# One program for the folded attention and the preparation of the quantised layers, with two loops in another order

## The reference, cut to what matters

```python
def _L1_xattn_ref(x, context, w_qkv, w_proj, b_proj):      # 16 heads of 8 channels; 257 context keys + 32 own
    q, k, v = split(x @ w_qkv.T)
    extra_k, extra_v = split(context)
    k = concatenate([extra_k, k]); v = concatenate([extra_v, v])
    attn = softmax((q * scale) @ k.T)
    return (attn @ v) @ w_proj.T + b_proj

def _L2_attn_ref(x, Wq, bq, Wk, bk, Wv, bv, temperature):
    q = (x @ Wq + bq).reshape(b, h, dh, t)                  # a reshape without a transpose: the "folded" layout
    k = (x @ Wk + bk).reshape(b, h, dh, t)
    v = (x @ Wv + bv).reshape(b, h, dh, t)
    attn = softmax(einsum('bhdt,bhds->bhts', k, v) * temperature)
    return einsum('bhdt,bhts->bhds', q, attn).reshape(b, t, d)

def _L2_ffn_ref(x, w1, b1, w2, b2):
    def _quant_per_tensor(x):
        scale = max(max(abs(x)), 1e-6) / 127                # one scale for the whole tensor
        return round(x / scale), scale
    def _qlinear(x2d, w, b):
        xq, sx = _quant_per_tensor(x2d); wq, sw = _quant_per_tensor(w)
        return (xq @ wq.T + b) * (sw * sx)
    return _qlinear(gelu(_qlinear(x, w1, b1)), w2, b2)
```

## Time and profile before

| | |
|---|---|
| three runs, us | 3599.93, 3603.46, 3603.1; median 3603.1 |
| the profiled execution's own time, us | 3595.71 |
| its span, first to last instruction, us | 3593.9 |
| busy, share of the span | PE 90%, DVE 70%, ACT 51%, POOL 35% |
| granted TensorE clock, mean | 0.933 |

### The profile page before, as it was taken

How to read it: one execution, slowest core, us unless ns; L and a number is a source line. 1 busy time by engine, 2 the same in 40 slices (tenths; PEclk the granted TensorE clock), 3 DMA queues, 4 the chain that set the end, 5 groups by cost and what they waited for, 6 DMA issues and landing times. The chain is left out here.

```text
span 3593.9 us, 110060 instructions
## 1 busy us (share of the span) xinstructions
PE 3239.3 (90%) x41584; PEld 2701.9 (75%) x41584; DVE 2516.7 (70%) x7222; ACT 1816.6 (51%) x4562; POOL 1252.0 (35%) x1855
## 2 busy tenths in 40 slices
PE   6887999999899999888899999999999999774866
PEld 4666999999867777546789899988998899543345
DVE  6785999999868888567455555555555555477765
ACT  4332777787677777574433333333333333224463
POOL 4774888888733333204200000000000000155042
PEclk8996999999999999998799999999999999877677
DMA  4001000000022222100465555555555555264000
GB/s 120 8 2 39 1 0 0 0 0 0 4 80 77 79 77 79 44 1 7 99 148 126 130 134 128 132 130 133 126 129 137 126 133 130 67 107 71 0 3 27
DMA packets 375654, 254.59 MB, mean 71 GB/s; under 512 B 118724, under 2 KB 371608, under 8 KB 374680
## 3 DMA queue, kind: packets, MB, share of 16 engines
q1 hardware_dynamic: 370968, 245.64, 28.1%
q10 hardware_dynamic: 4352, 4.20, 0.5%
HBM read 233.73 MB, written 15.75 MB: 69 GB/s over the span
## 5 line engine op out<-in xcount | busy, mean ns | idle before, releaser
L2477 PE MATMUL psum<-L_xattn_ctxT,L_xattn_q_ctx 128*128 128x257 f32 x2048 | 508.6, 388 | 2.5 <-issue 2.0
L1076 PE MATMUL psum<-L_ffn_share,L_ffn_prob 128*128 128x128 f32 x4096 | 488.1, 278 | 22.9 <-DVE L_ffn_prob L1009 15.4
L893 POOL TENSOR_TENSOR L_ffn_sums<-L_ffn_sims 128x1024 f32<-128x1024 f32 x256 | 485.4, 1913 | 61.2 <-DVE L_ffn_prob L1009 61.2
L2508 PEld LDWEIGHTS psum<-L_xattn_probT,L_xattn_ctx 32*128 32x128 f32 x16384 | 469.1, 187 | 44.5 <-issue 42.0
L1076 PEld LDWEIGHTS psum<-L_ffn_share,L_ffn_prob 128*128 128x128 f32 x4096 | 471.4, 193 | 35.7 <-DVE L_ffn_prob L1009 25.5
L2508 PE MATMUL psum<-L_xattn_probT,L_xattn_ctx 32*128 32x128 f32 x16384 | 493.5, 273 | 2.1 <-DVE L_xattn_probT L2391 2.1
L2329 ACT ACTIVATE L_xattn_prob<-psum,L_xattn_nmax 128x258 f32<-128x258 f32 x512 | 239.1, 472 | 478.1 <-DVE L_xattn_nmax L2377 461.1
L2300 POOL TENSOR_TENSOR L_xattn_z_var<-L_xattn_z_mv,L_xattn_z_eps 128x1 f32<-128x1 f32 x32 | 6.1, 192 | 1244.7 <-DVE L_xattn_z_mv L2403 1215.4
L2477 PEld LDWEIGHTS psum<-L_xattn_ctxT,L_xattn_q_ctx 128*128 128x128 f32 x2048 | 367.2, 190 | 64.4 <-issue 7.9
L935 ACT ACTIVATE psum<-L_ffn_sums,L_ffn_bias 128x512 f32<-128x512 f32 x512 | 339.1, 686 | 64.8 <-DVE L_ffn_prob L1009 60.3
L1009 DVE SCALAR_TENSOR_TENSOR L_ffn_prob<-L_ffn_sums,L_ffn_best,psum 128x512 f32<-128x512 f32 x512 | 358.1, 741 | 7.0 <-ACT psum L935 3.4
(11 more groups left out here) (461 smaller groups left out, 6521.8 us busy)
## 6 DMA issues: line engine op xcount, KB each, us to landing
L_xattn_ctx<-ctx_dram SPq DMA_DIRECT2D x512, 256.0 KB, 3.7
L_xattn_ctxT<-ctx_T_dram SPq DMA_DIRECT2D x128, 257.0 KB, 3.3
L_xattn_k_all<-ctx_T_dram SPq DMA_DIRECT2D x128, 128.5 KB, 2.1
L_xattn_v_all<-ctx_dram SPq DMA_DIRECT2D x128, 128.0 KB, 2.2
L_attn_qkv_scratch<-L_attn_qkv SPq DMA_DIRECT2D x24, 256.0 KB, 2.9
L_attn_rows<-L_attn_qkv_scratch SPq DMA_DIRECT2D x24, 256.0 KB, 5.3
start_raw<-ctx_dram ACTq DMA_DIRECT2D x16, 256.0 KB, 12.0
L_xattn_v_rows<-L_xattn_v SPq DMA_DIRECT2D x8, 256.0 KB, 2.3
```

What stands on the lines that cost most here:

```text
L893: nc.gpsimd.tensor_tensor(sums[:, h % RING, :, :], sx, sy, ALU.add).then_inc(summed, 1)
L1076: last = nc.tensor.matmul(pair(2 * s)[:, c * P:(c + 1) * P], prob[:, h % RING, c * P:(c + 1) * P], share[:, h % RING, :], start=(h == 0 an ...
L2477: last = nc.tensor.matmul(scores(s)[:, g, 0:CTX], q_ctx[:, p, c, b, h:h + 4, :].rearrange("p h n -> p (h n)"), ctxT[:, b, c, :], start=(c ...
L2508: last = nc.tensor.matmul(mix_bank(r)[:, c * P:(c + 1) * P], ctx[rows, b, k, c * P:(c + 1) * P], probT[rows, b % 2, k, :, :].rearrange("p ...
```

## The change

Four things are edited.

1. In `context_attention` TensorE's `turn` is split in `turn_upper` and `turn_lower`, and `mix_values` of the sequence before stands between them.
2. In `folded_attention`'s projection TensorE issues the transpose of a tile ahead of the matmul of the tile before it. The normalisation moves from VectorE to ScalarE, and GpSimd makes one more operand for it (mean times inverse deviation, negated).
3. What `quantised_ffn` did ahead of its first layer moves into `folded_attention`'s program, in a class `QuantisedFront`. The weights are loaded at its start; peaks and bias parts are made in the projection's last step, the rounding of the weights between the two loops; the six small transfers stand in SyncE's queue between `store_res(1, 1)` and `load_back(0, 0)`, their load after the loop over pairs.
4. At the end VectorE adds the results in five groups (8, 8, 8, 4, 4 tiles), each followed by its moments; GpSimd, ScalarE and the peaks follow by the same groups. The tile `back` is now a part of `qkv`.

```diff
@@ context_attention, TensorE @@
-                    turn(t, b)
+                    turn_upper(t, b)
                     if b:
                         mix_values(t, b - 1, before)
                     elif before:
                         mix_values(t - 1, BT - 1, before)
+                    turn_lower(t, b)
...
+class QuantisedFront:
+    PARTS = (range(0, 8), range(8, 16), range(16, 24), range(24, 28), range(28, 32))
...
+    def sp_send_parts(self, sp):
+        H, C = self.H, self.C
+        sp.wait_ge(self.parts_done, 3)
+        for i in range(3):
+            sp.dma_start(self.bias_dram[i:i + 1, 0:H].rearrange("a (p j) -> (a p) j", j=C), self.b_part[:, i, 0:C]).then_inc(
+                self.parts_out, 16)
+            sp.dma_start(self.bias_dram[i:i + 1, H:H + D].rearrange("a (p j) -> (a p) j", j=1),
+                         self.b_part[:, i, C:self.N_BIAS]).then_inc(self.parts_out, 16)
...
+    def sp_load_parts(self, sp):
+        sp.wait_ge(self.parts_out, 96)
+        sp.dma_start(self.bq[:, :], self.bias_dram).then_inc(self.bq_in, 16)
+
+    def pool_factors(self, pool):
+        for part in self.PARTS:
+            self.front.pool_rstd(pool, 0, only=part)
+            self.front.pool_shift(pool, self.shifted, part).then_inc(self.centred, 1)
...
@@ folded_attention @@
-        back = sb("back", [P, TILES, D])
+        back = qkv[:, :, 0, :]
...
             store_res(1, 1)
+            quant.sp_send_parts(sp)
             load_back(0, 0, back_in)
...
+            quant.sp_load_parts(sp)
             for n in (STEPS - 2, STEPS - 1):
                 store_res(n, n % 2)
-                load_back(n - 1, 1 - n % 2, back_in)
+                load_back(n - 1, 1 - n % 2, mid_in if n == STEPS - 1 else back_in)
             load_back(STEPS - 1, 1, last_in)
...
-            def rstd(t, j, live):
+            def normal_factors(t, j, live):
                 if live(-1):
-                    front.pool_rstd(pool, t + 1 - (j + 1) % W, only=(j + 1) % W)
+                    s = (j + 1) % W
+                    front.pool_rstd(pool, t + 1 - s, only=s)
+                    pool.drain()
+                    nc.gpsimd.tensor_scalar(shifted_mean[:, s:s + 1], front.mv[:, s, 0:1], front.rstd[:, s, :], -1.0, ALU.mult,
+                                            ALU.mult).then_inc(centred, 1)
...
@@ folded_attention, ScalarE @@
             def turn_copy(t, j, live):
-                front.act_copy(act, t - j, only=j)
+                if live(0):
+                    front.act_copy(act, t - j, only=j)
+                if live(-1):
+                    s = (j + 1) % W
+                    act.wait_ge(centred, t + 2)
+                    nc.scalar.activation(front.xn[:, s, :], core.x[:, ds(t + 1, 1), :].rearrange("p a d -> p (a d)"),
+                                         ACT.Identity, bias=shifted_mean[:, s:s + 1],
+                                         scale=front.rstd[:, s, :]).then_inc(front.normed, 1)
...
@@ folded_attention, VectorE @@
-                if live(-1):
-                    front.dve_normalise(dve, t + 1 - (j + 1) % W, only=(j + 1) % W)
...
+                if not live(-2) and live(-1):
+                    quant.dve_weight_peaks(dve)
+                    quant.dve_split_bias(dve)
...
             pipelined(dve, W, -1, 1, project)
+            quant.dve_greatest(dve, 1, 3, 1)
+            quant.dve_steps(dve, 1, 3, 1)
+            quant.dve_round_weights(dve)
             pipelined(dve, W, 0, 2, step)
-            dve.wait_ge(back_in, 16 * (STEPS - 1))
-            most = slice(0, TILES - S)
-            nc.vector.tensor_tensor(core.x[:, most, :], core.x[:, most, :], back[:, most, :], ALU.add)
+            dve.wait_ge(back_in, 16 * (STEPS - 2))
+            for part in quant.PARTS[0:3]:
+                add_back(part[0], part[-1] + 1)
+                quant.dve_moments(dve, part)
+            dve.wait_ge(mid_in, 16)
+            add_back(TILES - 2 * S, TILES - S)
+            quant.dve_moments(dve, quant.PARTS[3])
+            quant.dve_peak(dve, 0)
             dve.wait_ge(last_in, 16)
-            rest = slice(TILES - S, TILES)
-            nc.vector.tensor_tensor(core.x[:, rest, :], core.x[:, rest, :], back[:, rest, :], ALU.add)
+            add_back(TILES - S, TILES)
+            quant.dve_moments(dve, quant.PARTS[4])
+            for k in range(1, len(quant.PARTS)):
+                quant.dve_peak(dve, k)
+            quant.dve_step_x(dve)
...
@@ folded_attention, TensorE @@
+                if live(0):
+                    front.pe_transpose(pe, t - j, only=j)
                 if live(1):
...
-                if live(0):
-                    front.pe_transpose(pe, t - j, only=j)
...
             pe.wait_ge(qkv_done, TILES)
+            quant.pe_greatest(pe, 1, 3, quant.peaks_w, 1)
+            pe.wait_ge(quant.steps_read, 1)
             pipelined(pe, W, 0, 3, step)
-
-
+            pe.wait_ge(res_done, TILES)
+            quant.pe_greatest(pe, 0, 1, quant.peaks_x, 2)
```

More of the change, by code:

```diff
@@ L2900, in turn_copy @@
                 nc.scalar.copy(qT[:, j, :, :], bank_a(j).rearrange("p (c w) -> p c w", c=C)).then_inc(hT_done, 1)
-            for k, c in enumerate(chunks):
-                act.wait_ge(centred, k + 1)
-                for t in c:
-                    front.act_normalise(act, shifted, t)
             pipelined(act, W, 0, 0, gelu)
```

274 lines of the change are left out of this document (136 added, 138 removed).

## The result

| | before | after |
| --- | --- | --- |
| median of the runs, us | 3601.5 (3594.4 to 3603.5, 4 runs) | 3560.5 (3558.7 to 3565.2, 4 runs) |
| the profiled execution's own time, us | 3595.71 | 3560.66 |
| its span, us | 3593.9 | 3558.9 |
| granted TensorE clock, mean | 0.933 | 0.942 |

The ratio is 0.9895, 95% interval 0.9883 to 0.9908, so 1.05% faster, 38 us; by the two medians it is 41 us. The same kernel measured a second time gave 0.9905 (0.9888 to 0.9921), 36 us by the medians. Forecast were 3545 in 3518 to 3575.

A forecast was written before the change was run, and what follows sets the result against it. Context attention was taken as bound by a chain through all engines, not TensorE alone. -30 - 13 + 7 - 19 = -55 against the profiled 3595.7 gave 3541; adding 4 towards the runs' median made 3545, range 3518 to 3575.

The forecast's parts named there:

- Context attention: Moving the mix between upper and lower transposes shortens context attention by 30 us, ends -44 and -18.
- The link: Context attention: chain through all engines tying two sequences' steps; each gets 0.69 us shorter, 64 of them 44 us, the ceiling.
- The change of shape: Context attention: TensorE changes shape four times a sequence instead of three; 128 x 0.20 = 26 us if all on the path.
- the 18 us: Context attention: the gain left if the array's drain at each change of tiling mode is paid in full.
- The 47.9 us: Context attention: VectorE's wait for the end of the mix, taken as a bound nearly as high as the 44 us ceiling.
- Rival 2: Context attention: change of shape paid in full, ScalarE's later copy takes the rest; gain 0 to 15 us, 3560 to 3575; 20%.
- Projection: Folded attention's projection: steps of 1.6 us instead of 2.15 give -17, new work before the second loop +4, net -13.
- the work between the loops: Between projection and second loop: bias parts, weight peaks and rounding of weights add +4 us, ends +2 and +7.
- Rival 3: Projection stays near 2 us a tile, ScalarE having two waits in a row; -3 instead of -13, 3555; 15%.
- Six small writes: Second loop: loads of rows behind the writes in SyncE's queue are held, the mask once late; +7 us, lower end 0.2.
- Rival 1: Second loop: loads are not held by the small writes; the sum is -62, 3538; 30%.
- The end: End of folded attention, additions in groups: rounding of tokens at 3307.2 instead of 3325.99, -19 us, ends -21 and -14.

## Why the prediction was right, and where its sizes were off

The time lies in the range, 15 us above the number. Faster was right. By the steps of the prediction:

**Context attention, -30 forecast, -21 measured.** The link is there: 0.22 of it alone gave 14.1 us, 64 x 0.22. The change of shape, which I took for the cost, is not one: its 0.20 us stands in the trace, and the stage gained the whole 14.1 with it in every sequence. By the Trainium skill, TensorEngine Tiling (Array Packing), under Key Properties in Tiling Modes, the drain exists, and the idle 0.20 and 0.17 us agree with it; the 18 us that I drew from it as the low end were no bound of this kind. What fell short is the gain, in both halves of the 64 links, which I had taken as alike. Without the projection a link gained 0.38 us and not 0.69: VectorE had waited only 0.30 us for the mix there, and that wait is gone (at 1202.34 it waits 0.21 for scores instead). The 47.9 us that I took as a bound for all links lie mostly in the others, 1.15 us each. With the projection a link gained 0.30: there ScalarE's wait, "some 0.1 us, more in the step with the projection", is 0.7 us, since the projection stands between the upper and the lower transposes too, which I had not added into the walk. 32 x (0.31 + 0.39) = 22 us are missing from the 44. ScalarE's 23.1 us of waiting are nearly the same number, but that is chance: they can explain no more than the 32 x 0.39 = 12 us of the links in which they fall. That this wait is what took those 12 is read from the trace; no kernel isolates it. Rival 2 (no more than 15, since both costs are paid) has ScalarE's later copy right and the change of shape wrong.

**Projection, -17 + 4 = -13 forecast, -14.4 measured.** Steps of 1.52 us instead of 1.6 make it -19.5, so the work between the loops cost 5.1 instead of 4: the bias parts, which I let 1.3 us be seen of, held up the last two additions by some 4 us. Rival 3 is out. The clock rose instead of falling; what raised it, no run isolates.

**Six small writes, +7 forecast, +15.5 measured.** The largest error, and of kind as well as size. The held loads are there: 18.5 us to land, as the rule of the Trainium skill (DMA: Bandwidth & Descriptors, Queues, rings and completion order) would have it, rows late by 3.5 us at the mask. SyncE's issue of the three loads took 18.26 us too, which that rule doesn't cover. But I priced only what waits for rows. The engines halted for 5.5 to 11 us by themselves, in every kernel with these writes in the loop, at three places and from two queues, and TensorE came back at the low clock. My range for this term ended at 6.9; without the writes the loop is back at 89.1 (87.9 before). What the term left out is the halt, put at nothing: some 8 us with the low clock behind it. The held rows, the other 6 or so, are near the +7. Rival 1 (loads not held) is out.

**The end, -19 forecast, -18.0 measured**, step by step as walked: 24.55 us against 24.

The two errors, 9 and 8.5 us, have the same sign and add up to most of the 20 us by which the sum is off (-35.0 against -55); 3.3 lie in a stretch that varies by itself. That the time is within the range owes something to its width, 57 us.

What stays open: what halts the engines. TensorE or the path of its signals is the likeliest place: in one kernel it stopped inside a group of matmuls, in four traces ScalarE and VectorE resumed together on instructions that wait for it, and in all five its increments are recorded 6 to 13 us behind the end of its matmuls, while signals from VectorE to GpSimd got through. Whether the matmuls themselves ran late, the records don't tell: their ends are modelled. In the trace of the kernel before, VectorE and ScalarE worked on through the first 13 us of the same writes (3302 to 3315), while nothing waited for TensorE behind its matmul of 3305.07. A fetch of instructions held behind the writes looks like a candidate in the trace after (one that comes 37 us after the first maximum without small writes came 51 us after it here), but it is no good one: its packet starts at 3214.45, 2.9 us after the engines went on, and with the writes ahead of the third load the next fetch was due only some 4 us after the halt began. No experiment isolates it. Not tried either: the projection of a tile behind the lower transposes, which by the links above should give back up to 12 us, an estimate.

## What to carry to other kernels

When a transfer moves into a busy loop, price it by what it does to everything in flight, not only to the load behind it: six writes in pieces of 2 and 8 bytes cost 15 us in the loop, one write of three rows nothing that could be measured. Where an instruction moves between two others, walk every link of the period by itself, the one that holds something extra above all: a wait of 47.9 us in the sum was 1.15 us in one link and 0.30 in the next, and neither gave the 0.69 that was walked for one. And a gap in a trace next to a change of mode is not a cost until a kernel with more such changes is slower.

## What the runs showed of the hardware

Small writes stop engines that have nothing to do with them: with six writes of 128 pieces of 2 or 8 bytes under way, all four engines were idle for 8.8 us, and the transfers moved 15 GB/s meanwhile. In the five traces with these writes in or just ahead of the loop, the work went on 15.2 to 17.6 us after the last of them was issued, wherever they stood (16.1 us in the trace after). Six writes of 128 pieces of 512 bytes did nothing of it.

Four operations of VectorE on 5 elements to a partition took 0.86 to 0.93 us each while GpSimd ran 128x512 multiplications, and each of them ended 0.02 to 0.03 us behind the end of one; at 3158.09, with GpSimd idle, the same took 0.17.

Changes of shape on TensorE show up to 0.39 us of idle ahead of the weight load (0.39 from scores to transposes, 0.20 from the mix to transposes, 0.17 from transposes to scores), and one more in each sequence cost nothing that could be measured, in a stage whose pace the chain through the engines sets.
